# Input products of three gates ahead of the wait for the hidden state, in the LSTM rounds of a four-layer graph network in float32

## What is computed

```python
h = jnp.maximum(_layernorm(x), 0.0)
x = x + _L0_gnn_ref(h, adj, ...)      # degree-normalised graph convolution, two batch norms
h = jnp.maximum(_layernorm(x), 0.0)
x = x + _L1_gnn_ref(h, adj, ...)      # two graph convolutions, then:
        for p in range(1, MAX_SKIP + 1):          # MAX_SKIP = 4
            wins = h[:, :nw * p, :].reshape(Bv * nw, p, Hd)
            # _lstm_last: p steps, zero state; gates i, f, g, o
            #   g = x_t @ Wih.T + h @ Whh.T + bias
            #   c = sigmoid(f) * c + sigmoid(i) * tanh(g);  h = sigmoid(o) * tanh(c)
            h = h.at[:, idx, :].set(last)         # every p-th row is replaced
x = x + _L2_gnn_ref(...)              # needs all eigenvectors U of a 64 x 64 Laplacian
x = x + _L3_gnn_ref(...)              # three graph convolutions with adj * adj
```

## Time and profile before

| | us |
|---|---|
| median of 3 runs | 989.63 (988.39 to 990.43) |
| profiled execution, its own time | 988.91 |
| its span, first to last instruction | 987.1 |
| PE busy in the span | 856.1 |
| DVE busy | 571.1 |
| ACT busy | 518.7 |
| POOL busy | 348.2 |

### The profile page before, as it was taken

The page is one execution under the profiler, slowest core; times in us unless marked ns, Lnnn a source line. Parts: engine busy times, 40 slices in busy tenths (PEclk is TensorE's granted clock), DMA queues, the critical chain, the costliest instruction groups (busy, mean ns, idle before and its releaser), DMA issues.

```text
span 987.1 us, 12434 instructions
## 1 busy us (share of the span) xinstructions
PE 856.1 (87%) x3721; PEld 565.4 (57%) x3721; DVE 571.1 (58%) x3070; ACT 518.7 (53%) x958; POOL 348.2 (35%) x412
## 2 busy tenths in 40 slices
PE   2687768599899989998698879778999999999998
PEld 1344433364568536774367534566758848848846
DVE  5899867779778986779887987105104204304101
ACT  0466456466666736665466545474564454544531
POOL 1233210246555644565556556562202202202000
PEclk9999979799999999999899989898999999999999
DMA  8000000000000000000000000000000100100101
GB/s 336 0 1 1 1 0 1 1 1 1 0 1 1 1 1 1 2 0 1 0 1 1 1 1 0 1 1 1 1 0 2 43 0 1 43 0 1 43 1 43
DMA packets 2963, 13.27 MB, mean 13 GB/s; under 512 B 464, under 2 KB 464, under 8 KB 2640
## 3 DMA queue, kind: packets, MB, share of 16 engines
q1 hardware_dynamic: 2896, 12.48, 3.1%
HBM read 8.28 MB, written 4.19 MB: 13 GB/s over the span
## 4 chain that ended last, share of the span: by engine, by line
PE 61%; DVE 29%; ACT 4%; POOL 3%; issue 2%; DMA 0%; SPq 0%; DVEq 0%; ACTq 0%; POOLq 0%
PE PS L450 60%; POOL BIG L979 2%; DVE ST L1657 2%; DVE stats L1629 2%; DVE X L1833 2%; DVE Fq L1439 1%; DVE seg L1440 1%; ACT T L798 1%; DVE mv L1636 1%; DVE stats L1608 1%; ACT T L854 1%; POOL sc L948 1%; DVE sc L1173 1%; DVE vcol L1170 1%; DVE S L1190 1%
## 5 line engine op out<-in xcount | busy, mean ns | idle before, releaser
L450 PE MATMUL PS<-BIG,wts 128*128 128x512 f32 (+2 forms) x952 | 344.8, 498 | 14.2 <-POOL BIG L979 10.8
L979 POOL TENSOR_TENSOR BIG<-BIG 128x256 f32<-128x256 f32 (+2 forms) x252 | 239.2, 956 | 171.8 <-ACT BIG L888 88.0
L450 PEld LDWEIGHTS PS<-BIG,wts 128*128 128x128 f32 x952 | 179.0, 193 | 138.2 <-issue 96.8
L888 ACT ACTIVATE BIG<-PS,lbias 128x256 f32<-128x256 f32 (+2 forms) x312 | 165.5, 559 | 115.8 <-PE PS L450 113.5
L450 PE MATMUL PS<-H,wts 128*128 128x256 f32 (+2 forms) x312 | 123.0, 498 | 10.8 <-POOL H L979 7.0
L1833 DVE TENSOR_TENSOR X<-X,PS 128x512 f32<-128x512 f32 x64 | 43.3, 680 | 138.2 <-PE PS L450 87.1
L790 ACT ACTIVATE BIG<-PS 128x1024 f32<-128x1024 f32 x64 | 65.6, 1024 | 88.4 <-PE PS L450 88.4
L450 PE MATMUL PS<-T,wts 128*128 128x512 f32 x192 | 103.1, 659 | 2.2 <-ACT T L790 1.8
L790 ACT ACTIVATE T<-PS 128x512 f32<-128x512 f32 x96 | 55.8, 594 | 92.0 <-PE PS L450 91.7
L798 ACT ACTIVATE T<-X,shift,rstd 128x128 f32<-128x128 f32 x192 | 78.4, 482 | 34.6 <-DVE shift L1645 34.6
L1852 DVE TENSOR_TENSOR T<-PS,wts 128x512 f32<-128x512 f32 x16 | 11.1, 692 | 142.8 <-PE PS L450 142.8
(11 more groups left out here) (313 smaller groups left out, 1262.1 us busy)
## 6 DMA issues: line engine op xcount, KB each, us to landing
X<-x_in SPq DMA_DIRECT2D x1, 4096.0 KB, 12.7
out<-X SPq DMA_DIRECT2D x16, 256.0 KB, 2.0
wts<-w_in SPq DMA_DIRECT2D x1, 3542.0 KB, 21.4
cst<-cst_in SPq DMA_DIRECT2D x1, 419.0 KB, 3.4
AA<-adj_in SPq DMA_DIRECT2D x2, 16.0 KB, 2.0
```

Source lines behind the costliest of these rows:

```text
L450: return nc.tensor.matmul(o, l, r, start=start, stop=stop)
L888: nc.scalar.activation(LB[:, q, {"i": I_, "g": G_, "f": F_, "o": O_}[g], 0:n], PS[:, 3 * q + rank[q] % 3, 0:n], ACT.Tanh if g == "g" else ...
L979: nc.gpsimd.tensor_tensor(out, a, b, op).then_inc(pool_set[q], 1)
```

## The change

In a round with s > 0, PE now issues the input products of the first three gates (i, g, f), waits only then for the hidden state, and issues the three recurrent products and the pair of the fourth gate. Rounds with s = 0 are as they were, as is the number of products. The modelled clock gets each product's time when that product is issued (1 + 1 in place of 2, and 1 + 0.25 in place of 1.25), so its sum is the same, and its steps are finer.

```diff
-                        elif p > 1:
+                        elif p > 1 and s == 0:
 
                             pe.wait_ge(pool_set[q], R_POOL.at(i, f"h{r - 1}"))
-                        for at, g in enumerate(gates(s)):
+
+                        def input_part(g):
                             m = len(rank[q])
                             rank[q].append(f"{g}{r}")
...
                             G = PS[:, 3 * q + m % 3, 0:n]
                             j = mm(G, wT("wihT", p, g), x, stop=(s == 0))
+                            spend(n * 4 / 2400)
+                            return G, j
+
+                        if s:
+
+                            ahead = [input_part(g) for g in gates(s)[:3]]
+                            pe.wait_ge(pool_set[q], R_POOL.at(i, f"h{r - 1}"))
+                        for at, g in enumerate(gates(s)):
                             if s:
+                                G, _ = ahead[at] if at < 3 else input_part(g)
                                 j = mm(G, wT("whhT", p, g), LB[:, q, HP, 0:n], start=False)
+                            else:
+                                _, j = input_part(g)
                             j.then_inc(pe_set[q], 1)
-                            spend(n * 4 * (2 if s else 1.25) / 2400)
+                            spend(n * 4 * (1 if s else 0.25) / 2400)
```

## The result

The changed kernel takes 999.94 us (median; 998.36 to 1001.62) beside 990.03 for the kernel before on the same chip. The ratio is 1.0104, with a 95% interval of 1.0089 to 1.0119: the change costs 10 us. The forecast was 982.6, with a range to 990; it is wrong in sign. The profiled execution took 998.36, its span is 996.6.

What follows compares the result with a forecast made beforehand. PE, busy 87% of the span, was taken as the bound, its idle time and slow stretches the source of gain. 2.2 + 1.0 + 4.5 + 0.8 - 1.5 = 7.0 us off 988.9 gave 981.9, as median 982.6; range 977 to 990.

Steps and rivals of the forecast that it cites:

- the small products earlier: PE's order: finer clock steps leave 3.4 us less LSTM work ahead of the reflections' last product, so DVE's chain runs earlier.
- the end of the chain: 580 to 625 us: closer small products lengthen the last wait, roots behind the chain shorten it; 0, bounds ±2.
- Reflections: 330 to 360 us: layer-norm work spread flatter over four reflections, 1.0 us gained; bounds +1.7 and -2.96.
- the slower rival: PE meets small products before DVE is ready, each blocking all of PE; +4.3 us, so 994; chance 0.12.
- Grid and layer norm: 430 to 491 us: 3.4 from the chain's earlier start, 1.1 from waits, roots and clock; 4.5 gained, bounds 0 and 10.7.
- Factorisation: 537 to 580 us: DVE needs 42.8 us while PE waits; the stretch holds 0.8 us more PE work, gained.
- the five roots: Grid and layer norm: long sixteen-column roots beside POOL, some 5 us together, move behind the grid's passes; about 1 counted.
- Covered waits: First products of s = 1 rounds: input products ahead cover three of six hidden-state waits, 2.2 us gained; bounds 0 and 5.35.
- late gates: Rounds with s > 0: gates i and g complete later, moving h by 0.3 to 0.4 us; 1.5 us lost.

Runs made afterwards that it cites:

- order-only kernel: Only the LSTM matmuls moved as in the change, with the modelled clock of before, against the kernel before: 985.27 us, ratio 0.996.
- three ahead at s = 1: Three input products ahead only in rounds with s = 1, old clock, against the kernel before: 985.31 us; with pace 7.60 in place of 7.45, 981.18 us.

## Why the prediction was wrong

**The sum over stages failed at "the small products earlier".** That step counted 3.4 us less LSTM work ahead of a small product as a chain that starts 3.4 us earlier, in the reflections, the grid and the factorisation (1.0 + 4.5 + 0.8), and took the end of the chain at 0. Work that is not ahead of the last small product is behind it. The chain's end did not move (620.5 and 620.8), and 18 more instructions lie behind it, at 3.62 / 16 = 0.23 us each 4.1 us; yet it is 52.7 against 45.5 us, 7.2 lost. The other 3.1 go with a slower granted clock. The stretch from the last EV product to the end of the LSTM, before and then after:

```profile
620.51:666.01 45.50, 38.01 (x148) 29.13 (x149) 1.25 (x7) 27.53 (x66) 27.48 (x37) 0.94 0.00 1
```

```profile
620.79:673.52 52.73, 45.34 (x166) 33.80 (x167) 4.11 (x19) 30.51 (x72) 32.68 (x43) 0.89 0.00 1
```

PE idles 7.5 and 7.4 us in them. The granted clock was 0.94 and 0.89, which is an estimated 0.06 x 45.5 = 2.7 and 0.11 x 52.7 = 5.8 us lost to the lower level. The balance to set up was the end of the chain plus the work behind it. With the old order the fine clock put 3.6 us more behind the chain (49.1 for 45.5) and brought its end forward by 4.4, which paid; with the moved one it put 7.3 behind (52.7 for 45.4) and the end came 1.9 later (620.8 for 618.9).

**Reflections: forecast +1.0, measured 3.3 later.** The last product of a reflection in the table (64x2) came at 425.2 for 421.9, and PE's LSTM work was 7.8 us late by the end of iteration 1. The layer norm's work was summed at 4.4 us at most per reflection from durations of before, as if they stayed; between 359 and 370 six of its instructions were held. The evidence that DVE waited for PE at 422 us said nothing about the reflections between 336 and 367 us, where PE waited and DVE's chain did not once wait for its products, in either kernel. Here the slower rival described what happened, "a small product blocks all of PE", with the right sign; it was priced at 3.4 us of waits, and they grew by 7.0 (5.2 to 12.2). Of that 2.7 came behind 340 us, where it had placed them, and 4.2 at 236 and 254.

**Grid and layer norm: forecast +4.5.** The roots did get short there (1 held in place of 5 between 450 and 560), and "cst,tmp" was waited for by DVE less: 7.41 for 8.56, where below 3 was named. But the shift came at 490.90 and not before 485.5, PE's first "BDP" product at 499.41 and not by 487, at the second grid product DVE waited 5.98 us for PE where it had waited 2.02, and the adds, which the prediction had noted "22 steps later in DVE's order", held PE for 7.68 in place of the 4.77 and 4.30 of the earlier trace rows. DVE's timeline of after, shift, "cst,tmp" and second grid product:

```profile
490.90 1.29 DVE L1633 SCALAR_TENSOR_TENSOR shift<-mv,rstd 128x16 f32<-128x16 f32 x1
...
499.59 0.22 DVE L1416 SCALAR_TENSOR_TENSOR sc<-PS,sc 128x1 f32<-128x1 f32 x1 [7.41 <-PE PS L450]
...
539.26 0.22 DVE L1416 SCALAR_TENSOR_TENSOR sc<-PS,sc 128x1 f32<-128x1 f32 x1 [5.98 <-PE PS L450]
```

PE's LSTM work in iteration 2 took 1.5 us less, but the chain gained only 1.2 between the reflections and the second grid product, from 3.3 late to 2.1 (539.26 for 537.15). **Factorisation: forecast +0.8.** DVE's 42.8 us held (42.4), and as it started late, "both_ways" came 1.7 late.

**The roots and POOL.** The Trainium skill (SBUF — State Buffer, "Who interferes with whom") has a DVE instruction with two SBUF inputs and a GpSimd instruction that reads SBUF, or a DVE instruction in a two-port mode and a GpSimd instruction, exclude each other; the trace agrees, down to the ends of each POOL instruction (367.0, 368.3, 369.6 against 367.02, 368.24, 369.58). The prediction used it for the five roots that it saw, in a stretch where it then came out right. It didn't ask which roots beside the reflections would be held, and whether the moved matmuls' rhythm of POOL would hold more of them.

**Covered waits (2.2) and late gates (1.5).** Five of the six waits went. The sixth, 1.39 at 605.39, was taken for one of a round with s = 1; it is one with s = 0, which the change leaves alone, and it stayed (1.40). So the term was 0.47 + 0.38 = 0.85 us and not 2.2, and its upper bound 3.96 and not 5.35. The wait at 259.38 came back three products later, as foreseen (269.14, 1.29); the one at 493.35 did not. The late gates cost less than written: 1.86 for 1.80 and 1.92 for 1.64 at s = 0, and 2.43 in place of 4.77. Together 0.7 was forecast for the order by itself; its run gained 4.7. Its profiled execution (988.40) lies 3 us above its median, so the trace can't show where all of that is; the end of the chain is 1.6 earlier in it.

**Slow clock.** The same wait of 1.92 us stands in the order-only kernel and in after, followed by twelve instructions, which are six products. Order only, then after (643.43, above: 4.20):

```profile
635.96 2.86 PE L450 MATMUL PS<-H,wts 128*128 128x256 f32 x12 [1.92 <-POOL H L990]
```

The granted clock of the 3.4 us behind it, in both (order-only first, then after):

```profile
635.90:639.30 3.40, 3.34 (x16) 2.96 (x16) 0.00 (x0) 2.05 (x6) 2.35 (x5) 1.00 0.00 0
```

```profile
643.40:646.80 3.40, 3.37 (x11) 2.81 (x12) 0.00 (x0) 2.03 (x6) 2.35 (x4) 0.70 0.00 0
```

1.00 and 0.70, which is time spent at the lower of the two levels (1.2 and 2.4 GHz); it costs 1.3 us here (4.20 for 2.86), and nothing in these two rows tells which it will be. The forecast had no term for slower stretches behind the chain, where they cost some 3 us.

## What to carry to other kernels

When small products for a second engine's chain stand in a busy engine's order, moving them earlier is a trade and no gain: set up the end of the chain plus the work that is left behind it, and count a move only if the chain itself comes forward. Code that places instructions by a modelled clock is part of every edit of that clock: run an order change first with the clock untouched, then tune the pace for it (here 985.3 with three ahead at s = 1 became 981.2). And before gates, tiles or gathers are bunched together, look at which other engine then runs without a pause, and who is held up by it.

## What the runs showed of the hardware

In the trace of after a DVE instruction of the layer norm with sixteen columns that began beside a POOL product was held to its end, 14 times of 14: 0.16 becomes 1.15 us, with one-input forms (rstd at 367.15) held as well as two-input ones, and one-column steps of 0.26 passing between. How costly it is depends on whether POOL pauses: three products of 1.27 us in a row caught three DVE instructions in a row. A wait of 1.92 us was followed by full clock in one kernel and by a clock of 0.70 over 3.4 us in another.
